# Two 8-wide attentions: query and key parts laid out by DMA, and one output bank for 16 heads

## The reference, cut to what matters

```
# layer 0 (causal); layer 1 has no mask, biases on q, k, v, a rope over 128 columns, and / sqrt(8)
q = rope((xn @ Wq.T).reshape(b, n, 16, 8).transpose(0, 2, 1, 3))   # k likewise, v without rope
scores = einsum('bhqd,bhkd->bhqk', q, k) * (1 / 8) + add_mask
out = einsum('bhqk,bhkd->bhqd', softmax(scores), v)
x = x + out.transpose(0, 2, 1, 3).reshape(b, n, 128) @ Wo.T + bo + int8_ffn(xn)
```

## Time and profile before

| | |
|---|---|
| median of 3 runs | 3822.79 us (3822.34 to 3822.97) |
| the profiled execution | 3823.26 us, its span 3822.0 us |
| PE, DVE, ACT, POOL busy over the span | 91%, 68%, 67%, 60% |
| PE busy from 100 to 530 us (layer 0's attention) | 429.29 of 430 us |
| PE busy from 640 to 1030 us (layer 1's attention) | 378.38 of 390 us |
| first to last `invert` of layer 0's attention | 90.38 to 558.45 us |
| the same of layer 1's | 616.40 to 1064.56 us |
| SP's queue from 100 to 1650 us | no DMA issued |

### The profile page before, as it was taken

The page is one execution under the profiler, slowest core; times in us unless marked ns, Lnnn a source line. Parts: engine busy times, 40 slices in busy tenths (PEclk is TensorE's granted clock), DMA queues, the critical chain, the costliest instruction groups (busy, mean ns, idle before and its releaser), DMA issues.

```text
span 3822.0 us, 75943 instructions
## 1 busy us (share of the span) xinstructions
PE 3464.6 (91%) x25419; PEld 2498.4 (65%) x25419; DVE 2589.7 (68%) x5632; ACT 2549.5 (67%) x8202; POOL 2294.3 (60%) x2126
## 2 busy tenths in 40 slices
PE   4999987999986399969999889999999999999997
PEld 3666655666654288856675657676777777776665
DVE  6666666777628566564443478777777777778876
ACT  3777765888733145555353368888888888888886
POOL 3565654666613056633020078888888888888885
PEclk8999997999998599989999989999999999999999
DMA  3000000000000000020000000000000000000000
GB/s 114 2 1 2 2 1 1 1 1 1 1 1 1 0 1 1 1 95 12 1 1 1 12 1 1 2 2 2 2 2 2 1 2 1 2 2 2 2 1 23
DMA packets 28062, 28.88 MB, mean 8 GB/s; under 512 B 3424, under 2 KB 24736, under 8 KB 27424
## 3 DMA queue, kind: packets, MB, share of 16 engines
q1 hardware_dynamic: 27680, 24.03, 2.1%
HBM read 21.92 MB, written 2.10 MB: 6 GB/s over the span
## 4 chain that ended last, share of the span: by engine, by line
PE 41%; POOL 5%; ACT 4%; DVE 3%; issue 2%; DVEq 0%; ACTq 0%; POOLq 0%
PE psum L1915 7%; PE psum L1930 7%; PE psum L1905 7%; PE psum L1953 4%; POOL attn_p L2272 3%; PE psum L1402 3%; ACT attn_p L2027 2%; PE psum L1862 2%; POOL attn_qf L2266 2%; PE psum L1327 2%; PE psum L1413 2%; PE psum L1474 1%; PE psum L1493 1%; PE psum L1307 1%; DVE attn_nm L2147 1%
## 5 line engine op out<-in xcount | busy, mean ns | idle before, releaser
L2027 ACT ACTIVATE attn_p<-psum,attn_nm 128x256 f32<-128x256 f32 x1536 | 709.6, 478 | 249.7 <-DVE attn_nm L2147 245.2
L2272 POOL TENSOR_TENSOR attn_p<-attn_p,attn_rinv 128x512 f32<-128x512 f32 x768 | 783.5, 1041 | 132.5 <-DVE attn_rinv L2154 132.5
L647 POOL TENSOR_TENSOR sb_a_p<-sb_a_p,sb_a_rinv 128x512 f32<-128x512 f32 x512 | 522.3, 1042 | 327.6 <-DVE sb_a_rinv L534 325.6
L592 ACT ACTIVATE sb_a_p<-psum,sb_a_nm 128x256 f32<-128x256 f32 x1024 | 472.6, 476 | 126.0 <-DVE sb_a_nm L527 125.9
L2147 DVE TENSOR_REDUCE attn_nm<-psum 128x2 f32<-128x512 f32 x768 | 490.9, 680 | 20.0 <-PE psum L1905 19.7
L1930 PE MATMUL psum<-attn_pt,attn_v 128*64 128x256 f32 x3072 | 416.3, 391 | 32.0 <-DVE attn_ql L2166 27.7
L1915 PEld LDWEIGHTS psum<-sb_kept,attn_p 128*128 128x128 f32 x3072 | 328.3, 140 | 164.0 <-issue 92.3
L1915 PE MATMUL psum<-sb_kept,attn_p 128*128 128x128 f32 x3072 | 426.9, 280 | 8.4 <-POOL attn_p L2272 8.3
L527 DVE TENSOR_REDUCE sb_a_nm<-psum 128x2 f32<-128x512 f32 x512 | 327.8, 682 | 19.1 <-PE psum L444 14.2
L2027 ACT ACTIVATION_READ_ACCUMULATOR attn_p<-psum,attn_nm 128x1 f32 x1536 | 319.8, 208 | 0.0
L1930 PEld LDWEIGHTS psum<-attn_pt,attn_v 128*64 128x64 f32 x3072 | 192.8, 136 | 180.1 <-issue 57.7
(11 more groups left out here) (407 smaller groups left out, 8471.5 us busy)
## 6 DMA issues: line engine op xcount, KB each, us to landing
sb_x<-in_L_attn_x SPq DMA_DIRECT2D x4, 512.0 KB, 6.1
sb_wg<-in_L_ffn_Wg SPq DMA_DIRECT2D x1, 2048.0 KB, 10.7
sb_wu<-in_L_ffn_Wu SPq DMA_DIRECT2D x1, 2048.0 KB, 15.5
out<-sb_x SPq DMA_DIRECT2D x4, 512.0 KB, 3.2
sb_a_p<-in_const SPq DMA_DIRECT2D x1, 1024.0 KB, 4.9
sb_table<-in_const SPq DMA_DIRECT2D x1, 1024.0 KB, 8.8
sb_table<-in_const SPq DMA_DIRECT2D x1, 986.0 KB, 6.5
sb_w<-in_L_ffn_W SPq DMA_DIRECT2D x2, 256.0 KB, 4.7
```

What stands on the lines that cost most here:

```text
L592: ins = act.activation(Pr[:, p % 3, e, t, :], S(p, e)[:, t * N:(t + 1) * N], ACT.Exp, bias=nm[:, p % 4, e, t:t + 1], accum_out=rsum[:, p % ...
L647: pool.tensor_tensor(P3, P3, spread(rinv[:, (p - 1) % 4, e, :], N), ALU.mult).then_inc(normed.sem, 1)
L2027: ins = act.activation(Pr[p % 3][:, e, t, :], S(p, e)[:, t * N:(t + 1) * N], ACT.Exp, bias=nm[:, p % 4, e, t:t + 1], accum_out=rsum[:, p % ...
L2272: pool.tensor_tensor(P3, P3, spread(rinv[:, p % 4, e, :], N), ALU.mult).then_inc(normed.sem, 1)
```

## The change

- `stack_up` and the matrix `stack` are gone. DVE writes `part_hi` and `part_lo` (now a pair of tiles each for q and k). SP writes the two (128 rows of 1 KB each) into a DRAM buffer `a8_spilled`, waits until they have landed, and reads them back as 64 rows of 4 KB, twice, into the rows of a new tile `a8_spread`. ACT casts this tile in one instruction of 128x1024 instead of two of 128x512 from PSUM; it does so at j = 4 for q and j = 6 for k, where it was at j = 2, 3, 6, 7.
- The projection of k moves from j = 4 to j = 2, its `hi_lo` from j = 5 to j = 3.
- The scale of q is folded into its cos and sin tables, so one DVE instruction of `hi_lo` (line 507) is gone.
- V is laid so that the heads of group i have their 8 columns at 8 i of their 32. All 16 heads add into one bank O; `copy_out` and its ACT instruction come once a batch (at j = 2 of the next), and `through_wo` is one product per 128 tokens instead of four.
- `prepare8` no longer loads `stack` and `dup`; the table in SBUF is longer by 1152 columns.

```diff
-    raw_in = c.load("stack", (stack_raw, c.const("stack")), (dup_raw, c.const("dup")))
...
-        for g in range(GQ8):
-            pe.matmul(c.banks[4][:, g * D:(g + 1) * D], dup_raw[:, g * P:(g + 1) * P], t.w0[:, 3, :], start=True, stop=True)
-            mm = pe.matmul(c.banks[5][:, g * D:(g + 1) * D], dup_raw[:, g * P:(g + 1) * P], w1["o"], start=True, stop=True)
-        mm.then_inc(made.sem, 1)
+        pe.matmul(c.banks[7][:, 0:D], perm, t.w0[:, 3, :], start=True, stop=True)
+        pe.matmul(c.banks[7][:, D:2 * D], perm, w1["o"], start=True, stop=True).then_inc(made.sem, 1)
...
-        act.wait_ge(*raw_in)
-        act.copy(t.stack[:, :, :, :].rearrange("p a g m -> p (a g m)"), stack_raw).then_inc(stack_cast.sem, 1)
...
             for t in range(TB):
-                for g in range(GQ):
-                    mm = pe.matmul(M[:, t * P:(t + 1) * P], oT[b % 2][:, g, t * P:(t + 1) * P], wo4[:, g, :],
-                                   start=(g == 0), stop=(g == GQ - 1))
+                mm = pe.matmul(M[:, t * P:(t + 1) * P], oT[b % 2][:, t * P:(t + 1) * P], wo, start=True, stop=True)
...
-            elif j in (2, 3):
-                stack_up(b, 0, j - 2)
-            elif j == 4:
+            elif j == 2:
                 project(b, 1)
-            elif j in (6, 7):
-                stack_up(b, 1, j - 6)
...
-            if p >= 2 and p % 2 == 0:
-                pe.wait_ge(*out_moved(p // 2 - 1))
+            if j == 0 and b:
+                pe.wait_ge(*out_moved(b - 1))
...
         def hi_lo(b, j):
             dve.wait_ge(*rotated(2 * b + j))
-            if b or j:
-                dve.wait_ge(*stacked(4 * b + 2 * j - 1))
-            if j == 0:
-                c.dve_own(dve.tensor_scalar(rot[:, :], rot[:, :], scale, None, ALU.mult))
-            c.dve_own(dve.tensor_copy(part_hi[:, :], rot[:, :]))
...
+            if b:
+                dve.wait_ge(*landed[j](32 * b - 1))
+            hi, lo = part_hi[j], part_lo[j]
+            c.dve_own(dve.tensor_copy(hi[:, :], rot[:, :]))
...
-        def lay(b, j, half):
-            act.wait_ge(*stacked(4 * b + 2 * j + half))
+        def lay(b, j):
+            act.wait_ge(*landed[j](32 * (b + 1) - 1))
             if b >= 2:
                 act.wait_ge(*scored((b - 1) * PB - 1))
-            act.copy((q, ks)[j][b % 2][:, 2 * half:2 * half + 2, :],
-                     M.rearrange("p (g n) -> p g n", g=2)).then_inc(laid.sem, 1)
+            act.copy((q, ks)[j][b % 2][:, :, :], spreads[j][:, :, :]).then_inc(laid.sem, 1)
...
+        for p in range(NP + 3):
             b, j = divmod(p, PB)
+            if b and j == 2:
+                copy_out(b - 1)
+            if 2 <= p < NP + 2:
                 move_even(p - 2)
...
+            if b + 1 < B and j in (4, 6):
+                lay(b + 1, j // 2 - 2)
...
+        for b in range(B):
+            for j in range(2):
+                box = tiles.spilled[j]
+                sp.wait_ge(*parted(2 * b + j))
+                for n, half in enumerate((part_hi[j], part_lo[j])):
+                    dst = bass.AP(tensor=box, offset=n * wide, ap=[[N, GQ], [2 * wide, ROW], [1, N]])
+                    sp.dma_start(dst, half[:, :].bitcast(F32)).then_inc(away[j].sem, 16)
+                sp.wait_ge(*away[j](32 * (b + 1) - 1))
+                if b:
+                    sp.wait_ge(*laid(2 * (b - 1) + j))
+                for n in range(2):
+                    if j == 0:
+                        src = bass.AP(tensor=box, offset=n * wide, ap=[[2 * wide, ROW], [0, 2], [1, wide]])
+                        dst = bass.AP(tensor=spreads[j], offset=n * wide, ap=[[2 * wide, 2 * ROW], [1, wide]])
+                    else:
+                        src = bass.AP(tensor=box, offset=0, ap=[[wide, 2 * ROW], [1, wide]])
+                        dst = bass.AP(tensor=spreads[j], offset=n * wide, ap=[[2 * wide, 2 * ROW], [1, wide]])
+                    sp.dma_start(dst, src).then_inc(landed[j].sem, 16)
```

More of the change, by code:

```diff
@@ L49, in const_columns @@
     c["turn"] = turn
-    c["cos0"], c["sin0"], c["cos1"], c["sin1"] = rope_tables()
+    for layer, (cos, sin) in enumerate((rope_tables()[0:2], rope_tables()[2:4])):
+        c[f"cosk{layer}"], c[f"sink{layer}"] = cos, sin
+        c[f"cosq{layer}"], c[f"sinq{layer}"] = cos * QK_SCALE[layer], sin * QK_SCALE[layer]
+    f = np.arange(P)
+    head, d = f // HD8, f % HD8
+    perm = np.zeros((P, P))
+    perm[f, 32 * (head % 4) + HD8 * (head // 4) + d] = 1.0
+    c["perm"] = perm
     c["ones"] = np.ones((P, P))
@@ L67, in const_columns @@
     return {k: np.ascontiguousarray(v, dtype=np.float32) for k, v in c.items()}
[L70 to L87, removed]
 def const_layout(columns):
@@ L324, in act_program @@
         act.copy(t.br1[:, :], c.banks[6][:, 2 * D:2 * D + 2])
-        act.copy(t.wo[0][:, :, :], four(c.banks[4]))
-        act.copy(t.wo[1][:, :, :], four(c.banks[5])).then_inc(kept.sem, 1)
+        for i in range(2):
+            ins = act.copy(t.wo[i][:, :], c.banks[7][:, i * D:(i + 1) * D])
+        ins.then_inc(kept.sem, 1)
     def pool_program():
@@ L334, in prepare8, with attention8 @@
     pool_program()
-    return kept.all(), stack_cast.all(), zeroed.all()
-def attention8(c, x, xnT, tiles, ready, w, wo4, rope, scale, bias, causal, beside=None):
+    return kept.all(), zeroed.all()
+def attention8(c, x, xnT, tiles, ready, w, wo, rope, bias, causal, beside=None):
     nc = c.nc
     pe, act, dve, pool, sp = nc.tensor, nc.scalar, nc.vector, nc.gpsimd, nc.sync
-    cos, sin = rope
     O, M = c.banks[6][:, 0:N], c.banks[7]
@@ L354, in attention8 @@
     rotated, parted = c.steps("rope_added", 2 * B), c.steps("hi_lo_parted", 2 * B)
-    stacked, laid = c.steps("qk_stacked", 4 * B), c.steps("qk_laid", 4 * B)
+    away, landed = ([c.steps(f"parts_{s}_{k}", 32 * B) for k in "qk"] for s in ("away", "landed"))
+    laid = c.steps("qk_laid", 2 * B)
     v_ready = c.steps("v_parted", TB * B)
@@ L360, in attention8 @@
     even, odd = c.steps("even_moved", NP), c.steps("odd_moved", NP)
-    out_moved, through, added = c.steps("out_moved", NG), c.steps("through_wo", B), c.steps("added", B)
+    out_moved, through, added = c.steps("out_moved", B), c.steps("through_wo", B), c.steps("added", B)
     def pe_program():
@@ L624, in act_program @@
                 exps(p, 1)
-            if p >= 3 and p % 2:
-                copy_out((p - 3) // 2)
     def pool_program():
@@ L647, in pool_program, with sp_program @@
                     pool.tensor_tensor(P3, P3, spread(rinv[:, (p - 1) % 4, e, :], N), ALU.mult).then_inc(normed.sem, 1)
-            if b + 1 < B and j in (0, 4):
-                rotate(b + 1, j // 4)
+            if b + 1 < B and j in (0, 2):
+                rotate(b + 1, j // 2)
+    def sp_program():
+        wide = GQ * N
+        for b in range(B):
+            for j in range(2):
+                box = tiles.spilled[j]
[14 more added lines that the diff above has]
+                    sp.dma_start(dst, src).then_inc(landed[j].sem, 16)
     pe_program()
```

106 lines of the change are left out of this document (44 added, 62 removed).

## The result

The changed kernel takes 3831.16 us, median of 15 runs, against 3822.79 for before. (One run of the 15 took 4983 us at a mean granted clock of 0.62; it is left out of the ratio.) The profiled execution took 3831.01 us.

The account below looks back on a forecast made before the run. DVE and ACT's 3.37 us per loop step was the floor, with PE making the excess above it. From 3823.3, -6 - 31 - 17 - 4.5 + 1 + 8 = -49.5 gives 3773.8, median 3773; range 3759 less 3, to 3804.

Parts of the forecast that it names:

- The floor: Attention loop: DVE and ACT close a ring of 3.37 us a step, 26.96 a batch, that no PE saving can pass.
- The gain of PE's work: Attention loops: less PE work brings batches to 27.4 us in layer 0 (-31 us) and 27.0 in layer 1 (-17).
- The lag of j = 0 and 2: Layer 0's projection steps: PE runs at most 0.67 us over the floor; 0.4 taken, bounds 0 and 0.7.
- The start: Before layer 0's attention: fewer loads, casts and dup products save 8.0 us, later big casts cost 1.9: -6.1 us.
- Layer 1's prologue: Before layer 1's first scores: stackings and casts go (-7.7 us), a DRAM trip of 7.9 and a cast come (+8.9): +1.2.
- the round trip: q's and k's parts through DRAM and back: 5.6 to 7.9 us, the later taken, each lay 0.3 late, +8 us.
- the window: Attention loop: time from q's or k's parts being ready until their cast must start three steps later, 7.6 us.
- A batch pays once: Attention loops: q's stall also pushes k's cast back, so each of 30 batches pays 0.3 us only once.
- The clock: Rival: PE idles up to 0.85 us a step, TensorE's clock falls to 1.2 GHz; 24 slow steps eat the gain; chance 0.01.
- a slow trip that stalls the ring: Rival, DRAM trip: each microsecond beyond 7.6 costs 30 us, slower than before past 9.5, 3852 at 10.5; chance 0.10.
- between 8.6 and 9.3, faster still: Rival case: a DRAM trip of 8.6 to 9.3 us leaves the kernel still faster than before; chance 0.10.
- no change: Rival case: a DRAM trip between the still faster and the slower cases leaves the time unchanged; chance 0.03.

Follow-up runs that it names:

- e1: The changed kernel with ACT's casts of q and k one step later, at j = 5 and 7: 3776.9 us, ratio 0.9875.
- e11: The changed kernel run again as it is, on the same chip as e10: 3829.2 us, ratio 1.0017.
- e5: e4 with each projection's two products put into neighbouring steps and the casts at j = 5 and 7: 3762.3 us, ratio 0.9841.
- e6: The changed kernel with q's parts copied from SBUF to SBUF in eight DMAs, without DRAM; k keeps its trip: 3819.1 us.
- e10: The changed kernel with unread PE products ahead of the weighing at j = 5 and 7, adding to their bank without restarting it: 3819.5 us, ratio 0.9992.
- the output half alone: The kernel before with one output bank, one copy per batch and one output product per tile; stackings and their casts stay: 3783.6 us, ratio 0.9896.
- the DMA half alone: The changed kernel with the four output groups of before (four copies, eight products, dup loaded): 3833.9 us, ratio 1.0028.
- e4: The changed kernel with the DRAM write's outer dimension 128 instead of 4, read back by four DMAs instead of two: 3775.1 us, ratio 0.9877.
- e2: The changed kernel with ACT's casts of q and k one step earlier, at j = 3 and 5: 3972.5 us.
- e7: The changed kernel with unread PE products ahead of the weighing at j = 5 and 7, which restart the sum of outputs: 3818.4 us.

## Why the prediction failed, step by step

- **The floor** was right: 3.37 us wherever nothing is late, 26.90 to 26.96 a batch.
- **The gain of PE's work** was right. Without a late cast (e1) layer 0 has 27.68 (forecast 27.4) and layer 1 26.95 (27.0). The lag of j = 0 and 2 was 0.7, the upper bound, since nearly none of it is absorbed: +5 us.
- **The start** gave 5.4 us (6.1 forecast). **Layer 1's prologue** cost more: k's cast starts 9.3 us behind its first issue, not 7.9. The stretch between the attentions grew by 2.1 us though the tail's 1.45 is in it: +3.6 instead of +1.2. **The rest** of the span, untouched, is 3.5 us longer after. Most of this need not be the change's: it is 0.6 us longer in e11, the same kernel, and in the profiled executions of the other experiments it lies between 0.8 us less (e5) and 4.8 more (e1). What varies there is open.
- **The failed step is the round trip**, "then each lay is 0.3 us late ... +8 us". The write on four engines was foreseen: 4.5 us for the hop, 4.80 measured. The second hop was priced as one load of 512 KB, 3.4 us. It is two DMAs, the issues take 0.6 us each, a read lands 3.0 us (2.8 to 4.8) behind its issue, and the cast came 8.9 - 4.8 = 4.1 us behind the first. So the trip is 8.9 us in the middle and up to 10.4, not 7.9; the cast, 1.04 instead of 0.95, takes another 0.1 from the window. With the prediction's own price of 30 us for each microsecond, 8.9 against the window of 7.6 makes 39 us. Measured: 32.2 us of waits in front of q's casts, and k's 9.6 on top, 41.8 together.
- **"A batch pays once"** was half right: k's cast waited in 15 batches for 9.6 us even behind q's stall, and for 32 when q's was gone (e6).
- **The clock** was named as a rival for the wrong cause, steady idle time, with 0.01. Idle times of up to 0.85 us, step after step, do no harm (layer 1 of e1: 1.00). The stalls' 1.9 to 2.8 us do: 9.7 us by e10 against e11.
- **In sum**: the attentions lost 52.3 us against e1's (18.7 + 33.6): 41.8 of waits, and the 10.5 that are left are about what e10 puts on the clock. The miss of the profiled execution is 3831.0 - 3773.8 = 57.2 us: 33.8 of waits beyond the 8 forecast, these 10.5, 5 of lag, 0.7 of the start, 2.4 of layer 1's prologue, 3.5 of the rest, which makes 56. The mechanism, a slow trip that stalls the ring, was among the rivals, at 30 us for each microsecond, but the measured trip of 8.9 us falls in its case "between 8.6 and 9.3, faster still" (0.10), which by that price ends at 3804. What came is the time of its next case, "no change" at 9.3 to 9.5 (0.03), since k's own waits and the clock had no term.

The mistake behind it: the window had no reserve, 7.6 against 7.9, and an estimate without spread was put on a serial chain of two DMAs with a semaphore wait between. What was left out of the chain, the second issue and the spread of the landings, could only lengthen it.

## What to carry to other kernels

- When a transfer takes the place of work on an engine, compare its whole chain (issues, first landing, reaction, second issues, landing) with its window, and leave a step of reserve: one step later was worth 54 us here, at no cost.
- Take halves of a change apart: the output half alone gave 40 us, the DMA half alone cost 11.
- Look at a DMA's outermost dimension: with 128 instead of 4 the same bytes were written 2.6 us sooner (2.2 us to the reads' first issue instead of 4.8).

## What was not expected of the hardware

- A dependent trip SBUF, DRAM, SBUF of 2 x 128 KB out and 2 x 256 KB back took 8.9 us in the middle, up to 10.4. With a wide write and four reads (e4) the reads' first issue comes after 2.2 us, and casts 7.5 to 8.0 us behind the first issue wait for 0.9 us in 30 batches.
- An issue on SP is not one price: 0.55 us for a write cut as 4 x 32 x 256, mostly 0.33 to 0.43 with 128 rows, 0.5 to 0.6 for a read, 0.6 for a copy within SBUF.
- After single idle stretches of PE of 1.9 to 2.8 us (after) and 4.1 to 6.7 us (e2) the granted clock fell to 1.2 GHz for 3.4 us and more, though once not after 2.6; products that nobody reads in these stalls kept it up, and paid (9.7 us).
- A product that starts in one half of a PSUM bank also restarts a sum that stands in the other half on the same rows (e7's outputs are off by a relative 0.84; in e10, which adds, they are right). The Trainium skill says so in "PSUM — Partial Sum Buffer", section "The four PSUM rules": a first matmul clears the written-bits of the whole 2 KB bank in the quadrants that it writes. The two runs agree with it.
